# A four-batch attention and expert kernel: input loads reordered over two queues, first tiles projected and rotated by a path of their own, values projected in step 0

## The reference, cut to what matters

```python
x = x + layernorm(attention(layernorm(x), Wq, Wk, Wv, Wo))
x = x + layernorm(ffn(layernorm(x), ...))
# attention: 16 query heads and 4 key/value heads of 64, rotary embedding on q and k
# (pairs of neighbouring rows turned by a cosine and a sine table), scores = q k^T / 8,
# causal mask, softmax, times v, times Wo
# ffn: linear, gated unit, 8 experts of which 4 are taken plus a shared part, linear, gated unit
```

## Time and profile before

| what | value |
|---|---|
| median of 3 runs | 1491.96 us (1490.4 to 1493.01) |
| the profiled execution | 1484.45 us |
| its span, first to last instruction | 1482.4 us |
| mean granted TensorE clock | 0.985 |
| TensorE matmul busy | 1333.7 us, 90% |
| VectorE, ScalarE, GpSimd busy | 981.0, 774.2, 407.7 us |

### The profile page before, as it was taken

How to read it: one execution, slowest core, us unless ns; L and a number is a source line. 1 busy time by engine, 2 the same in 40 slices (tenths; PEclk the granted TensorE clock), 3 DMA queues, 4 the chain that set the end, 5 groups by cost and what they waited for, 6 DMA issues and landing times.

```text
span 1482.4 us, 31001 instructions
## 1 busy us (share of the span) xinstructions
PE 1333.7 (90%) x10417; PEld 931.1 (63%) x10432; DVE 981.0 (66%) x2044; ACT 774.2 (52%) x1709; POOL 407.7 (27%) x412
## 2 busy tenths in 40 slices
PE   2699999899999988998999989999999899999996
PEld 1477677677676766876766668676766644444442
DVE  3677777664777768476777775777768257666665
ACT  2556666554566556365566554666665233333333
POOL 0343444322434424143434331434440000000000
PEclk9799999999999999999999999999999999999999
DMA  8211112110111110112111111111110000000000
GB/s 235 82 38 64 60 46 67 38 58 28 64 53 67 35 61 29 58 41 69 35 67 57 43 54 33 55 50 67 49 57 2 1 1 8 7 8 8 8 8 14
DMA packets 79028, 67.64 MB, mean 46 GB/s; under 512 B 39904, under 2 KB 62304, under 8 KB 78816
## 3 DMA queue, kind: packets, MB, share of 16 engines
q1 hardware_dynamic: 78944, 66.55, 13.8%
HBM read 7.81 MB, written 2.10 MB: 7 GB/s over the span
## 4 chain that ended last, share of the span: by engine, by line
PE 36%; POOL 14%; ACT 14%; DMA 12%; issue 10%; DVE 7%; SPq 4%; ACTq 1%; POOLq 0%; DVEq 0%
DMA turned<-raw 12%; POOL turned L907 7%; POOL roped L932 7%; PE rows L611 7%; ACT probs L716 7%; PE rows L422 6%; PE o_out L471 5%; PE o_out L634 3%; PE turn L441 3%; ACT raw L695 3%; SPq L315 3%; ACT probsT L725 2%; DVE neg_max L1046 2%; PE o_out L390 2%; PE proj_bank L390 1%
## 5 line engine op out<-in xcount | busy, mean ns | idle before, releaser
L1046 DVE TENSOR_REDUCE neg_max<-rows 128x1 f32<-128x768 f32 (+7 forms) x512 | 363.7, 752 | 226.6 <-PE rows L425 226.6
L716 ACT ACTIVATE probs<-rows,neg_max 128x768 f32<-128x768 f32 (+7 forms) x512 | 373.2, 734 | 89.3 <-DVE neg_max L1046 86.2
L471 PE MATMUL o_out<-probsT,v_g 128*64 128x128 f32 (+1 forms) x3328 | 278.5, 318 | 0.7 <-DVE probsT L1060 0.7
L471 PEld LDWEIGHTS o_out<-probsT,v_g 128*64 128x64 f32 x3328 | 201.5, 137 | 68.5 <-issue 19.6
L441 PE MATMUL turn<-cf,probs 128*128 128x128 f32 x1792 | 242.8, 276 | 1.3 <-DVE probsT L1060 1.1
L422 PE MATMUL rows<-kk,qh 64*128 64x512 f32 (+2 forms) x768 | 170.8, 441 | 80.7 <-ACT probs L716 74.6
L725 ACT ACTIVATE probsT<-turn 128x512 f32<-128x512 f32 x256 | 152.5, 596 | 142.2 <-PE turn L441 138.4
L441 PEld LDWEIGHTS turn<-cf,probs 128*128 128x128 f32 x1792 | 195.1, 143 | 1.9 <-DVE probsT L1060 1.3
L916 POOL COPY inv_wide<-inv_sum 128x256 f32<-128x256 f32 x128 | 50.9, 398 | 507.3 <-DVE inv_sum L1052 476.5
L422 PEld LDWEIGHTS rows<-kk,qh 64*128 64x128 f32 x768 | 72.4, 185 | 168.2 <-ACT probs L716 120.3
L1060 DVE COPY probsT<-turn 128x512 f32<-128x512 f32 x256 | 174.5, 682 | 1.5 <-PE turn L441 1.1
(11 more groups left out here) (154 smaller groups left out, 1677.8 us busy)
## 6 DMA issues: line engine op xcount, KB each, us to landing
turned<-raw SPq DMA_DIRECT2D x192, 128.0 KB, 2.0
kk<-kk SPq DMA_DIRECT2D x16, 512.0 KB, 2.9
kl<-kl SPq DMA_DIRECT2D x16, 512.0 KB, 3.7
v_g<-v_all SPq DMA_DIRECT2D x32, 256.0 KB, 3.0
slab_a<-w_qk SPq DMA_DIRECT2D x16, 256.0 KB, 2.6
xm<-in_x SPq DMA_DIRECT2D x4, 512.0 KB, 7.4
slab_b<-w_qk SPq DMA_DIRECT2D x16, 128.0 KB, 2.2
out<-xm SPq DMA_DIRECT2D x8, 256.0 KB, 2.3
```

What stands on the lines that cost most here:

```text
L471: ins = mm(dst, v_g[p][:, t, :], x, start=t == 0, stop=t == big_w - 1)
L716: A(probs[:, s % 2, q * 128:q * 128 + width], rows[h][:, 0:width], ACT.Exp, bias=neg_max[:, s % 2, item:item + 1], accum_out=exp_sum[:, s ...
L1046: V.tensor_reduce(neg_max[:, s % 2, item:item + 1], rows[h][:, 0:width], AX_X, ALU.max, negate=True).then_inc(max_ready, 1)
```

## The change

What it does:

- The loads are split by need over two queues. SP issues x of batch 0, the small part of cf, wq of groups 1 to 3, wv, cosines and sines, cb. ACT's own queue issues wq of group 0 and the two copies of wk. x of batches 1 to 3 and the twenty weights are issued by SP after `w_split`, in front of step 0. The epsilon column of cf moves ahead of the cosines, which then begin at column 257 instead of 256.
- VectorE makes the moments of x first. Weights are converted and split in two portions: group 0 ahead of the tokens' low parts, all others (with w_v) behind the first rotations.
- TensorE projects the first four tiles straight from `w_qk`. slab_a isn't loaded for them.
- These four tiles have four `turned` and four `roped` buffers (two of each lie in the space of the probabilities). The swaps wait only for the eviction of their tile.
- The values of batch 0 are projected in step 0, as in the other batches.
- One load of an activation table, ahead of step 0, is gone, and one moves forward.
- The semaphore for x of batches 1 to 3 becomes one for each batch; VectorE waits for it in step 0.

```diff
-C_ID, C_ONES, C_TIE, C_COS, C_SIN, C_EPS, C_F32 = 0, 128, 192, 256, 256 + S, 256 + 2 * S, 257 + 2 * S
+C_ID, C_ONES, C_TIE, C_EPS, C_COS, C_SIN, C_F32 = 0, 128, 192, 256, 257, 257 + S, 257 + 2 * S
...
+        first_roped = [roped[:, 0, :], roped[:, 1, :], ninth[5], ninth[6]]
+        first_turned = [turned[:, 0, :], turned[:, 1, :], ninth[7], ninth[8]]
...
# SP
-            sp.dma_start(xm[:, 0:TILES, :], x_v[0]).then_inc(x0_loaded, 16)
-            sp.dma_start(cf[:], io["cf"]).then_inc(consts_in, 16)
-            sp.dma_start(cb_raw, io["cb"]).then_inc(consts_in, 16)
+            sp.dma_start(xm[:, 0:TILES, :], x_v[0]).then_inc(x_in[0], 16)
+            sp.dma_start(cf[:, 0:C_COS], io["cf"][:, 0:C_COS]).then_inc(small_in, 16)
...
-            sp.dma_start(wr[:, :, 0:64], wk).then_inc(w_in, 16)
-            sp.dma_start(wr[:, :, 64:128], wk).then_inc(w_in, 16)
-            sp.dma_start(wr[:, :, 128:384], io["wq"].rearrange("p (g n) -> p g n", g=HKV)).then_inc(w_in, 16)
+            sp.dma_start(wr[:, 1:HKV, 128:384], io["wq"].rearrange("p (g n) -> p g n", g=HKV)[:, 1:HKV, :]).then_inc(w_in, 16)
             sp.dma_start(w_raw[:, HKV * 384:HKV * 384 + 256], io["wv"]).then_inc(w_in, 16)
+            sp.dma_start(cf[:, C_COS:], io["cf"][:, C_COS:]).then_inc(consts_in, 16)
+            sp.dma_start(cb_raw, io["cb"]).then_inc(cb_in, 16)
...
-            for b in range(1, B):
-                sp.dma_start(xm[:, b * TILES:b * TILES + TILES, :], x_v[b]).then_inc(x_loaded, 16)
-            for dst, src in loads:
-                sp.dma_start(dst, src).then_inc(ffn_w_in, 16)
-            sp.wait_ge(w_split, 1)
...
-                for k in range(PROJ_A if b == 0 else 0):
-                    swap_pairs(b, 0, k)
...
-            first_slabs()
+            for k in range(PROJ_A):
+                sp.wait_ge(raw_kept, k + 1)
+                for odd in range(2):
+                    sp.dma_start(first_turned[k][odd:128:2, :], raw[1 - odd:128:2, k, :]).then_inc(swapped_first[k], 16)
+            sp.wait_ge(w_split, 1)
+            move(slab_b[:], w_qk[:, :, 0, 256:384]).then_inc(slab_b_in, 16)
+            for b in range(1, B):
+                sp.dma_start(xm[:, b * TILES:b * TILES + TILES, :], x_v[b]).then_inc(x_in[b], 16)
+            for dst, src in loads:
+                sp.dma_start(dst, src).then_inc(ffn_w_in, 16)
             for b in range(B):
                 batch(b)
# TensorE
+            def project_first(k, dst):
+
+                n, c = k // 2, half_of(k)
+                pe.wait_ge(x_split, c + 1)
+                split_product(dst, [w_qk[:, a, 0, n * 128:n * 128 + 128] for a in range(2)],
+                              [xT[:, a, c * HALF:c * HALF + HALF] for a in range(2)], proj_done)
...
-                if first and s == 0:
-                    turn_kept(pe, step_index(b, 0, 0) - 1, MOVES - 2)
-                    turn_kept(pe, step_index(b, 0, 0) - 1, MOVES - 1)
+                if isinstance(g, int) and g == 0 and s == 0:
+                    if b:
+                        turn_kept(pe, step_index(b, 0, 0) - 1, MOVES - 2)
+                        turn_kept(pe, step_index(b, 0, 0) - 1, MOVES - 1)
+                    else:
+                        pe.wait_ge(w_split, 1)
                     project_values(b)
                     pe.wait_ge(v_kept, 4 * b + 4)
...
-            pe.wait_ge(x_split, 2)
+            pe.wait_ge(w_first, 1)
             for k in range(PROJ_A):
-                project(0, 0, k, rows[k % 2][:, k // 2 * HALF:k // 2 * HALF + HALF])
-            project_values(0)
-            pe.wait_ge(v_kept, 4)
+                project_first(k, rows[k % 2][:, k // 2 * HALF:k // 2 * HALF + HALF])
+            pe.wait_ge(cb_ready, 1)
# ScalarE
+            act.dma_start(wr[:, 0, 128:384], io["wq"][:, 0:256]).then_inc(w_first_in, 16)
+            for n in (0, 64):
+                act.dma_start(wr[:, :, n:n + 64], wk).then_inc(w_first_in, 16)
+            nc.scalar.preload_act_table_set("natural_log_exp_and_others")
+            act.wait_ge(small_in, 16)
+            inverse_deviations(0, 0, TILES)
+            act.wait_ge(w_first_in, 48)
             A(w_qk[:, 0, :, 0:128], wr[:, :, 0:128], ACT.Copy, scale=float(D) ** -0.5)
-            A(w_qk[:, 0, :, 128:384], wr[:, :, 128:384], ACT.Copy)
-            A(w_v[:, 0, :], w_raw[:, HKV * 384:HKV * 384 + 256], ACT.Copy).then_inc(w_high, 1)
...
+            A(w_qk[:, 0, 0, 128:384], wr[:, 0, 128:384], ACT.Copy).then_inc(w_high, 1)
             for a in range(2):
                 keep_tokens(0, a, turn_bank[a])
+            act.wait_ge(w_in, 32)
+            A(w_qk[:, 0, 1:HKV, 128:384], wr[:, 1:HKV, 128:384], ACT.Copy)
+            A(w_v[:, 0, :], w_raw[:, HKV * 384:HKV * 384 + 256], ACT.Copy).then_inc(w_high, 1)
             for k in range(PROJ_A):
                 keep_raw(0, 0, k, rows[k % 2][:, k // 2 * HALF:k // 2 * HALF + HALF])
...
-            nc.scalar.preload_act_table_set("natural_log_exp_and_others")
+            act.wait_ge(cb_in, 16)
+            A(cb[:], cb_raw, ACT.Copy).then_inc(cb_ready, 1)
+            for k in range(PROJ_A):
+                cols = slice(half_of(k) * HALF, half_of(k) * HALF + HALF)
+                act.wait_ge(rope_sum, k + 1 + ROPES_G)
+                A((kk[0] if k < 2 else qh[0])[:, cols], first_roped[k], ACT.Copy).then_inc(rope_high, 1)
# VectorE
+                    if b + 1 < B:
+                        dve.wait_ge(x_in[b + 1], 16)
                     moments(lambda t: next_tokens(b)[:, t, :], range(TILES), 0).then_inc(var_ready, 1)
...
-            dve.wait_ge(w_high, 1)
-            V.scalar_tensor_tensor(out=w_qk[:, 1, :, 0:128], in0=wr[:, :, 0:128], scalar=float(D) ** -0.5,
-                                   in1=w_qk[:, 0, :, 0:128], op0=ALU.mult, op1=ALU.subtract)
...
-            dve.wait_ge(x0_loaded, 16)
+            dve.wait_ge(x_in[0], 16)
             moments(lambda t: xm[:, t, :], range(TILES), 0).then_inc(var_ready, 1)
             refine(0, 0, TILES)
             for t in range(TILES):
                 normalise(x_norm1[:, t, :], xm[:, t, :], t).then_inc(ln_done, 1)
...
+            dve.wait_ge(w_high, 1)
+            split_weights(0, 1).then_inc(w_first, 1)
             for a in range(2):
                 split_tokens(0, a, turn_bank[a])
+            dve.wait_ge(consts_in, 16)
...
+            for k in range(PROJ_A):
+                first_cos(k)
+                if k == 1:
+                    first_sum(0)
+            for k in range(1, PROJ_A):
+                first_sum(k)
+                first_low(k - 1)
+            first_low(PROJ_A - 1)
+            dve.wait_ge(w_high, 2)
+            split_weights(1, HKV)
+            V.tensor_tensor(w_v[:, 1, :], w_raw[:, HKV * 384:HKV * 384 + 256], w_v[:, 0, :], ALU.subtract).then_inc(w_split, 1)
```

More of the change, by code:

```diff
@@ L190, in build @@
         up_g, up_u, gate_bank, y_bank, side = score, block_max[0:2], block_max[2], o_bank[0], [o_bank[1], m_bank]
[L193 to L196, removed]
+        cb_ready, small_in, cb_in = map(sem, ("cb_ready", "small_in", "cb_in"))
+        x_in = [sem(f"x_in{b}") for b in range(B)]
+        consts_in, w_first_in, w_in, ffn_w_in, out_stored = map(
+            sem, ("consts_in", "w_first_in", "w_in", "ffn_w_in", "out_stored"))
+        swapped_first = [sem(f"swapped_first{k}") for k in range(PROJ_A)]
+        w_high, w_first, w_split = map(sem, ("w_high", "w_first", "w_split"))
         slab_a_in, slab_b_in, k_copied, spacer = map(sem, ("slab_a_in", "slab_b_in", "k_copied", "spacer"))
@@ L350, in batch @@
             def batch(b):
-                for k in range(PROJ_A if b == 0 else 0):
-                    swap_pairs(b, 0, k)
                 steps(sp, b, lambda g, s, last, depth: step(b, g, s, last))
-            first_slabs()
+            for c in range(2):
+                sp.sem_inc(swapped[c], 32 * (PROJ_A // 2))
+            for k in range(PROJ_A):
[8 more added lines that the diff above has]
+                sp.dma_start(dst, src).then_inc(ffn_w_in, 16)
             for b in range(B):
@@ L781, in step @@
                     keep_raw(b, g + ahead, k, proj_bank)
-                if first and s == 0 and b:
+                if first and s == 0:
                     keep_values(b)
-            act.wait_ge(consts_in, 32)
-            A(cb[:], cb_raw, ACT.Copy).then_inc(cb_ready, 1)
-            act.wait_ge(w_in, 64)
             wr = w_raw[:, 0:HKV * 384].rearrange("p (g n) -> p g n", g=HKV)
-            A(w_qk[:, 0, :, 0:128], wr[:, :, 0:128], ACT.Copy, scale=float(D) ** -0.5)
-            A(w_qk[:, 0, :, 128:384], wr[:, :, 128:384], ACT.Copy)
@@ L800, in _ @@
+            A(w_v[:, 0, :], w_raw[:, HKV * 384:HKV * 384 + 256], ACT.Copy).then_inc(w_high, 1)
             for k in range(PROJ_A):
                 keep_raw(0, 0, k, rows[k % 2][:, k // 2 * HALF:k // 2 * HALF + HALF])
-            for k in range(2):
-                keep_high(0, 0, k)
-            keep_values(0)
-            for k in range(2, PROJ_A):
-                keep_high(0, 0, k)
```

(31 more changed lines are left out.)

26 lines of the change are left out of this document (10 added, 16 removed).

## The result

| | before | after |
|---|---|---|
| median of the runs of this comparison | 1492.49 us (1490.4 to 1494.42, 4 runs) | 1472.54 us (1468.57 to 1475.47, 4 runs) |
| profiled execution | 1484.45 us, span 1482.4 | 1475.47 us, span 1473.6 |
| ratio | 1 | 0.9865 [0.9838, 0.9892] |

The gain is 20 us (16 to 24 by the interval). The forecast was 8.1 us and 1483.9, the range 1478.5 to 1490: the prediction was wrong, on the fast side.

The account below looks back on a forecast made before the run. TensorE is busy for 90% of 1482.4 us, but three delays one behind the other hold up its start. Terms -16.2 + 0 + 8.1 = -8.1 us, from 1491.96 to 1483.9 us; range 1478.5 to 1490.

Parts of the forecast that it names:

- the column's: Tables moved from column 256 to 257: taken at 0; rival that GpSimd's sine products get slower, chance 0.06.
- SP's queue: One slab and 23 loads issued by SP in front of step 0: 15 us, lowest 11, highest 20.
- Part 5: SP's late loads delay tile 4's swap in step 1: ScalarE waits 6.3 us, high part at 54.25, 8.1 us earlier than before.
- that backlog: 1.7 MB still under way behind SP's 23 loads in the kernel before, some 5 us at 313 GB/s.
- The full-queue rival: SP's loads in front of step 0 take the full 20 us: 5 us less gain, 1488.9 us, chance 0.14.
- everything after keeps its distance: After tile 4's high part in step 1, the 8.1 us lead carries on unchanged to the end.
- The front: Start up to the first projection: x lands at 5.6 us, TensorE projects at 12.9 us instead of 29.08.
- part 1: Loads by need at the start: first projection 16.2 us earlier, with the slabs' 6.60 us of idle time included.
- The own buffers: Separate buffers for the four first tiles: give nothing, 15.7 us from first projection to first scores as before.
- The exclusion: First rotations: two-SBUF-input VectorE and GpSimd operations run one after the other, 15.7 us; if merely shared, 12.0.
- The values in step 0: All of batch 0's values projected in step 0: +3.6 us, lying beside the wait for tile 4.
- x of batch 1: Late load VectorE waits for in step 0: needed 8.7 us after first scores, landing about 8, so has room.

Follow-up runs that it names:

- experiment 2: Kernel before the change with only the new column order (tables from column 257 instead of 256): 1474.63 us, ratio 0.9904 to the kernel before.
- experiment 1: Changed kernel with its sine and cosine tables back at a multiple of 256 columns (512 instead of 257): 1487.9 us, ratio 0.9995 to the kernel before.
- experiment 7: Changed kernel with the four first cosine products reading their tile from PSUM instead of its SBUF copy: 1472.78 us, a single run.
- experiment 8: Changed kernel with tables at column 512 and SP's late weight loads spread in portions of four, four and twelve: 1476.42 us, ratio 0.9925 to the kernel before.
- experiment 4: Changed kernel with 56 GpSimd and 12 VectorE products added at its end, varying the operands' column offsets: 1551.64 us, a single run.
- experiment 5: Changed kernel with only the buffer of the sums (roped) moved by three columns: 1453.07 us, ratio 0.9763 to the kernel before.
- experiment 6: Changed kernel with its cosine and sine tables beginning at column 259 instead of 257: 1483.57 us, a single run.
- experiment 3: Changed kernel with SP's late loads spread, four weights behind tile 4's swap, seven behind the value slices, nine behind tile 5's swap: 1468.84 us, ratio 0.9853 to the kernel before.

## Why the prediction was wrong

Two terms of the sum failed, in opposite directions: the column's, put at 0, and that of SP's queue, put at 15 us.

**The column, taken at 0, is nearly all of the net gain.** "I take 0: type and step of the operands stay, and a shift by 4 bytes of 1024 is nearer to the lower bound." The trace of before had no such operand, and the bounds were written as 0 and 1.27 us: a loss was priced, a gain left out without any reason that excludes one. An unknown rate has two sides. With the lower side open, the same sentence that prices a loss (92 products on the path, 12 us for 10%) prices the gain: 14% measured, 14.3 us (experiment 2). The place was right (sine product on the path between swap and ScalarE), the sign wasn't considered. The forecast's chance for the column, 0.06, stood on the slower side alone.

**Part 5's -8.1 us became -0.7 (experiment 1, 2.4 to either side).** Where it went, by the traces:
- *SP's queue, 15 us.* Measured 18.9 us to the key copy. The sentence "that backlog was some 5 us" took off what was already under way in before. But the DMA engines have the same bytes to move, and the stretch of 19 us is 97% busy at 242 GB/s, not the 313 of the earlier trace rows. The 23 loads that took 19.65 us before take 18.2 here. The full-queue rival had this at 20 us and was the nearest; it stood at 0.14. The swap behind the queue is late twice, by its own issue (0.98 a part) as well. With 1.4 us won before (first scores 27.19), the high part came at 56.10 with products of 1.09 us and at 57.45 with 1.26 (experiment 1), for a forecast of 54.25.
- *The clock behind the wait.* The forecast said "everything after keeps its distance". After 9 us without work TensorE got 0.50, then 0.78 of its clock. In experiment 1 it got 0.50 up to 61.5 us and 0.73 up to 66.0, and the lead over before, which had 1.00 from 62 us on, is 4.9 us at the high part of tile 4 and 3.8 one step on.
- *Later swaps.* That lead falls to 2.6 us at the inversion of step 6 (105.88 against 103.31), since a transfer that in before's trace had landed quickly didn't. The swap ahead of it and who waits for it, by the timeline of before:

```profile
98.39 1.12 SPq L315 DMA_DIRECT2D turned<-raw  x2
101.36 1.29 POOL L907 TENSOR_TENSOR turned<-turned,cf 128x512 f32<-128x512 f32 x1 [1.74 <-DMA turned<-raw]
104.10 0.63 ACT L704 ACTIVATE qh<-roped 128x512 fp32r<-128x512 f32 x1 [2.71 <-POOL roped L932]
```

And by that of experiment 1:

```profile
94.36 1.11 SPq L307 DMA_DIRECT2D turned<-raw  x2
98.80 1.28 POOL L919 TENSOR_TENSOR turned<-turned,cf 128x512 f32<-128x512 f32 x1 [3.21 <-DMA turned<-raw]
101.53 0.63 ACT L715 ACTIVATE qh<-roped 128x512 fp32r<-128x512 f32 x1 [4.18 <-POOL roped L944]
```

  2.97 us from issue to product before, 4.44 here. But experiment 2, which has the old start, needs 4.57 (97.61 to 102.18) and ScalarE waits 4.13 us there; the other traces, the changed kernel's too, have 3.5 to 4.2. So the new start isn't the cause: before's profiled execution, one of its quickest, was the lucky one. This item tells two traces apart; it is nothing that the change did. Why the swap was quick there is open.

**What held.** The front: x at 5.24 for 5.6, first projection at 12.67 for 12.9, the 16.2 us of part 1 (29.08 less 12.67 is 16.4). By the Trainium skill (DMA: Bandwidth & Descriptors, "Issuing engines are not separate DMA queues") ScalarE's loads share the sixteen engines with x. Here x landed 4.4 us after its issue instead of 4.1, and VectorE started at 5.24, near the early end of the bounds. The own buffers: 15.2 us from first projection to first scores with products of 1.26 us (experiment 1: 12.86 to 28.01) for 15.7 forecast and 15.7 before. The exclusion behind this is what the Trainium skill (SBUF — State Buffer, "Who interferes with whom") states. The trace agrees (3.08 us for two products of 0.69), and so does experiment 7. The values in step 0 were covered: step 1's first scores wait 0.69 us for them at 41.00, and ScalarE's wait for tile 4 sets the time. x of batch 1 was not late. So the path was named right and its largest term was mis-sized; with SP's queue taken apart, the start gives 11.2 us (experiment 8), near the 12.6 that 16.2 less 3.6 make.

Open: why the relative position of two inputs matters, and whether the values ahead of step 0 would have been better, which wasn't tried. Of the 7.4 us between forecast and experiment 1, the queue's 3.2 (8.1 less 4.9) and the clock's 1.1 (4.9 less 3.8) are read from single traces; what takes the other 3 isn't shown, and 2.4 of them could be noise.

## What to carry to other kernels

- When a layout moves operands, even by four bytes, put the instruction's rate into the sum with a gain and a loss. On GpSimd, let the second input of a product or sum on the path begin 1 or 2 columns (fp32) past the first, modulo 4; the order counts, since 1 column before it is 3 and slow. Three columns of pad gave 15 us for the sum alone.
- Loads that are "not needed yet" aren't free if the queue that they sit in also issues what a step waits for. Put a few behind each urgent transfer: 23 ahead of one cost 10 us here, and seven ahead of the next took most of that gain back. Count such a queue by its bytes at the rate that it gets, not by its issues.
- Undo the parts of a change one by one even if the sum looks right: here a term of -14 and a term of -0.7 would have passed for a start that gives 15 to 20 us.

## What the runs showed of the hardware

- GpSimd's 128x512 fp32 product or sum of two SBUF inputs takes 1.09 us if the second input begins 1 or 2 columns past the first modulo 4, and 1.26 if 0 or 3 (experiments 1, 2, 4, 5, 6). VectorE's takes 0.69 us in the three positions tried. The Trainium skill (GPSIMD Engine Reference, "Performance versus the Vector engine") gives about 2.6 cycles for an element of a two-input operation, since both inputs take turns at one read port. By its 1.2 GHz that makes an estimate of 1.11 us for 512 elements; the 1.09 agrees, and the 1.26 is 14% above it. By the Trainium skill (Advanced Engine Details and Errata, "SBUF Cachelines") SBUF is read in lines of 16 bytes, which is the period seen; no run here shows that this is the cause.
- SP's issue of a transfer takes longer with much queued ahead. In the changed kernel's queue (4.6 MB moved in 19 us) the load of w_o took 1.58 us and each part of the swap 0.98; in experiment 3, where the loads were spread, 0.59 and 0.55 (at 39.27 and 38.12).
- Two VectorE products of 0.69 us took 3.08 us beside GpSimd's, and 1.28 us with one of their inputs in PSUM (experiment 7).
- After a stretch of 9.6 us with 0.50 us of TensorE work the granted clock was 0.50 for 1.9 us and 0.78 over the next 4 (58.10 to 64.00 us of the changed kernel).
